# Self-attention projections in three rounded rounds, w2's sums behind attention, ternary clips split between VectorE and GpSimd

## The reference

```python
Xn = (X - mu) * rsqrt(var + LN_EPS) * ln_w + ln_b
Q, K, V = split(Xn @ W_in, 3);  Q, K = rope(Q), rope(K)      # 512 x 1536
out = softmax(Q K^T / sqrt(32)) V @ W_out + X
...
def act_quant(x):    # per token
    scale = 127.0 / clip(max(abs(x)), EPS); return clip(round(x * scale), -128, 127) / scale
def weight_quant(w): # one scale for a whole matrix
    scale = 1.0 / clip(mean(abs(w)), EPS);  return clip(round(w * scale), -1.0, 1.0) / scale
def bitlinear(x, w): return act_quant(x) @ weight_quant(w).T
h = silu(bitlinear(x, w1)) * bitlinear(x, w3);  return bitlinear(h, w2)   # 512 -> 1408 -> 512
```

## Time and profile before

| | us |
|---|---|
| median of 3 runs | 554.95 (554.63 to 555.12) |
| the profiled execution | 555.15 |
| its span, first to last instruction | 553.4 |
| PE busy in the span | 526.5 |
| DVE busy | 450.5 |
| ACT busy | 364.7 |
| POOL busy | 148.7 |

### The profile page before, as it was taken

One profiled execution on the slowest core, in us unless ns is written; L12 is line 12 of the kernel. 1 busy time (PEld: TensorE's weight loads), 2 busy tenths in 40 slices (PEclk: granted clock), 3 DMA queues, 4 the chain that ended last, 5 costly groups with the idle time before them and its releaser, 6 DMA issues.

```text
span 553.4 us, 10020 instructions
## 1 busy us (share of the span) xinstructions
PE 526.5 (95%) x3831; PEld 353.1 (64%) x3835; DVE 450.5 (81%) x650; ACT 364.7 (66%) x445; POOL 148.7 (27%) x202
## 2 busy tenths in 40 slices
PE   6989998799999999999999999999998899998996
PEld 3757763367666666767666676766677686454543
DVE  3354995999999999999999999999998833569686
ACT  2124535887887787788788688688688614995442
POOL 2367953002202202202202202202100001596500
PEclk9999999899999999999999999999999999999999
DMA  8999288999999999999999999999999987700001
GB/s 305 350 358 306 106 141 261 232 205 184 209 191 205 199 197 198 211 212 204 207 204 195 202 205 195 199 207 196 203 191 197 153 333 277 322 0 1 1 2 38
DMA packets 288350, 107.93 MB, mean 195 GB/s; under 512 B 276928, under 2 KB 278464, under 8 KB 286912
## 3 DMA queue, kind: packets, MB, share of 16 engines
q1 hardware_dynamic: 288320, 107.54, 89.6%
HBM read 37.79 MB, written 0.52 MB: 69 GB/s over the span
## 4 chain that ended last, share of the span: by engine, by line
PE 78%; DVE 10%; ACT 5%; DMA 4%; issue 2%; SPq 1%; ACTq 0%; DVEq 0%
PE ps L679 19%; PE ps L681 9%; PE ps L661 9%; PE ps L662 9%; PE ps L663 9%; PE ps L711 4%; PE ps L722 3%; DMA keys<-ctxT 2%; DVE rows L1300 2%; PE ps L788 2%; PE ps L733 2%; DVE split L1272 2%; PE ps L629 1%; PE ps L631 1%; PE ps L630 1%
## 5 line engine op out<-in xcount | busy, mean ns | idle before, releaser
L679 PE MATMUL ps<-pT,VH 128*128 128x256 f16 x1024 | 195.7, 273 | 3.7 <-DMA pT<-split 3.7
L681 PE MATMUL ps<-pT,VL 128*128 128x128 f16 x1024 | 182.6, 219 | 0.0
L1300 DVE TENSOR_SCALAR_CACHE_REDUCE rows<-ps,qback 128x1024 f32<-128x1024 f32 x128 | 163.6, 1280 | 17.8 <-PE ps L663 17.4
L1052 ACT ACTIVATE split<-rows,rz 128x2048 f16<-128x2048 f32 x64 | 124.6, 1995 | 67.7 <-DVE rz L1240 67.6
L1272 DVE SCALAR_TENSOR_TENSOR split<-rows,rz,split 128x2048 f16<-128x2048 f32 x64 | 150.1, 2348 | 2.9 <-ACT split L1052 2.1
L679 PEld LDWEIGHTS ps<-pT,VH 128*128 128x128 f16 x1024 | 100.4, 98 | 44.0 <-DMA pT<-split 5.7
L1038 ACT ACTIVATE rows<-rows,negm 128x2048 f32<-128x2048 f32 x64 | 127.2, 1988 | 0.2 <-DVE negm L1305 0.2
L681 PEld LDWEIGHTS ps<-pT,VL 128*128 128x128 f16 x1024 | 100.4, 98 | 27.3 <-issue 0.4
L542 POOL TENSOR_TENSOR ctx_c<-acc 128x128 f32<-128x128 f32 x32 | 23.9, 748 | 296.5 <-ACT acc L1027 296.5
L661 PE MATMUL ps<-KH,qcur 128*128 128x512 f16 x256 | 97.5, 381 | 3.3 <-DVE rows L1300 3.3
L662 PE MATMUL ps<-KL,qcur 128*128 128x512 f16 x256 | 97.5, 381 | 0.0
(11 more groups left out here) (187 smaller groups left out, 622.7 us busy)
## 6 DMA issues: line engine op xcount, KB each, us to landing
w_sb<-w SPq DMA_DIRECT2D x3, 2816.0 KB, 15.6
wq_sb<-wq SPq DMA_DIRECT2D x4, 1024.0 KB, 8.1
wo_sb<-wo SPq DMA_DIRECT2D x16, 256.0 KB, 5.3
wkcq_sb<-wkcq SPq DMA_DIRECT2D x4, 768.0 KB, 9.7
keys<-ctxT SPq DMA_DIRECT2D x8, 256.0 KB, 8.6
stage<-ctxT SPq DMA_DIRECT2D x16, 128.0 KB, 9.0
stage<-kcos SPq DMA_DIRECT2D x8, 256.0 KB, 9.1
stage<-ksin SPq DMA_DIRECT2D x8, 256.0 KB, 9.6
```

The source lines that it names most:

```text
L679: nc.tensor.matmul(bank(6 + r % 2, 0, 256), VH[:, 4 * b + k, :], p.rearrange("p x q -> p (x q)"), start=(b == 0 and k == 0), stop=False)
L681: last = nc.tensor.matmul(bank(6 + r % 2, 0, 128), VL[:, 4 * b + k, :], p[:, 0, :], start=False, stop=(b == 7 and k == 3))
L1052: nc.scalar.activation(split[:, split_slot(r, half), :, 0, :], rows[:, k, half * 2048:(half + 1) * 2048].rearrange("p (b k) -> p b k", k=1 ...
L1300: nc.vector.tensor_scalar(rows[:, k, c * 1024:(c + 1) * 1024], ps[:, score_bank(s) * 512:(score_bank(s) + 2) * 512], qback[:, r // 2:r // ...
```

## The change

The projections become three rounds on `float32r` operands. ScalarE rounds the three weights and the normalised tokens (`qkv_weight_high`, `normalised_high`), DVE subtracts for the low parts (`qkv_weight_low`, `normalised_low`), and DVE takes over scale and shift from ScalarE (`normalised`). TensorE's order becomes one of 72 products in groups (`project` with `highs` and `lows`). The loads of the key and query weights no longer wait for the last product of cross-attention, only for the last turned probabilities.

The residual of self-attention is rounded to a high and a low part on GpSimd, and added by two products with a rounded identity instead of an fp32 one.

The sums of w2 move from the time of the projections and scores to behind the last copy of probabilities, its total behind the last context, and its scale into the layer norm of tile 0, ahead of that norm's reciprocal. w1's clip on DVE becomes four quarters, one in each of the pairs 2 to 5, and w3's whole clip stands behind pair 5's context. w2's clip becomes eight pieces on GpSimd, two ahead of its multiplication for tile 0 of `hmid` and six behind it; each down product waits for its piece. GpSimd's wait for two clips and the ten dummy products are gone.

```diff
+    CLIPS = (4, 1)
...
-            sp.wait_ge(av_done, 16 * XH)
-            sp.dma_start(wink_sb[:, :, :], w_k).then_inc(win_in, 16)
-            sp.dma_start(winq_sb[:, :, :], w_q).then_inc(win_in, 16)
-            sp.dma_start(winv_sb[:, :, :], w_v).then_inc(win_in, 16)
+            for c in range(4):
+                sp.wait_ge(pt_in[c], 16 * 2 * XH)
+            sp.dma_start(wink_sb[:, :, :], w_k).then_inc(win_in[0], 16)
+            sp.dma_start(winq_sb[:, :, :], w_q).then_inc(win_in[1], 16)
+            sp.wait_ge(av_done, 16 * XH)
+            sp.dma_start(winv_sb[:, :, :], w_v).then_inc(win_in[2], 16)
...
+                nc.gpsimd.tensor_copy(x2hi[:, t, :], x_sb[:, t, :]).then_inc(x2hi_done, 1)
+                pool.wait_ge(x2hi_done, t + 1)
+                nc.gpsimd.tensor_tensor(x2lo[:, t, :], x_sb[:, t, :], x2hi[:, t, :].bitcast(f32), ALU.subtract)\
+                    .then_inc(x2lo_done, 1)
...
-            pool.wait_ge(wclip_done, 2)
             weight_magic(2, w2_sb)
             weight_round(2, w2_sb, w2b)
+            def last_clips(first, end):
+                for k in range(first, end):
+                    part = slice(k * DK * FF // WPIECES, (k + 1) * DK * FF // WPIECES)
+                    pool.wait_ge(wround_done, WPIECES * 2 + k + 1)
+                    nc.gpsimd.tensor_scalar(w2b[:, part], w2b[:, part], 1.0, -1.0, ALU.min, ALU.max).then_inc(w2clip_done, 1)
+
+            last_clips(0, 2)
             for t in range(TT):
                 a, b = HPARTS[1]
                 pool.wait_ge(hscale_done, t + 1)
                 nc.gpsimd.tensor_scalar(hmid[:, t, a:b], hmid[:, t, a:b], qscale[:, t:t + 1], MAGIC, ALU.mult, ALU.add)\
                     .then_inc(hmagic_done, 1)
+                if t == 0:
+                    last_clips(2, WPIECES)
...
-            project(0, 0)
+            project(0, 0, "weight", True, False)
             pe.wait_ge(x1_done, TT)
-            project(0, 1)
+            project(0, 1, "weight", True, False)
+            project(0, 0, "token", None, True)
+            project(0, 1, "token", None, True)
             pe.wait_ge(z1_done, 2)
             tile_transposes(z1[:, 1, :], 1, zT_done)
-            project(0, 2)
+            project(0, 2, "token", True, False)
+            project(1, 0, "weight", True, False)
+            project(0, 2, "weight", None, True)
+            project(1, 0, "token", None, True)
             weight_sum(0, bank(7, 0, 1))
-            project(1, 0)
-            project(1, 1)
...
-                if v == 2:
-                    weight_sum(2, bank(3, 0, 1))
+                if v == 0:
+                    pe.wait_ge(v_copied, 2)
+                    weight_sum(1, bank(3, 0, 1))
...
+                if t == 0:
+                    weight_sum(2, bank(0, 0, 1))
...
-            keep_busy(10, 2)
             quantised_transposes(0)
...
+                        if t == 0:
+                            pe.wait_ge(w2clip_done, -(-(c + 1) * DM // (DK * FF // WPIECES)))
...
+            for c in range(4):
+                abs_sum(2, c)
...
+            def qkv_weight_low(j):
+
+                dve.wait_ge(win_hi_done, j + 1)
+                nc.vector.tensor_tensor((wink_lo, winq_lo, winv_lo)[j][:, :, :].rearrange("p c d -> p (c d)"),
...
+            residual(0)
+            two_layernorms(0)
+            qkv_weight_low(0)
+            qkv_weight_low(1)
+            normalised(0)
+            normalised_low(0)
+            residual(1)
+            two_layernorms(1)
+            normalised(1)
+            qkv_weight_low(2)
+            normalised_low(1)
...
             rotate(0, 0)
+            rotate(0, 1)
             weight_total(0)
-            rotate(0, 1)
             value_copies(0)
+            rotate(1, 0)
             weight_scale(0, bank(7, 0, 1))
-            rotate(1, 0)
-            weight_total(1)
             rotate(1, 1)
-            weight_scale(1, bank(7, 0, 1))
...
-                if v in (2, 3):
-                    clip(v - 2, (w1b, w3b)[v - 2])
+                if v in (2, 3, 4, 5):
+                    clip(0, w1b, v - 2)
                 if v in (3, 5, 7):
                     context_out(v // 2 - 1)
+                if v == 5:
+                    clip(1, w3b, 0)
             context_out(FG - 1)
-            clip(2, w2b)
+            weight_total(2)
...
-                layernorm(x_sb, h2, t, t + 1, bank(6 + t), x3_done)
+                layernorm(x_sb, h2, t, t + 1, bank(6 + t), x3_done, between=(lambda: weight_scale(2, bank(0, 0, 1))) if t == 0 else None)
```

More of the change, by code:

```diff
@@ L152, in program @@
         acc = small("acc", [128, 2, 2, 128])
+        hTn_hi = at("hTn_hi", off[0], [128, TT, DK, 128], f32r)
         cT = small("cT", [128, FG, TOK])
@@ L291, in program @@
         warm_done = sem("warm_done")
-        wclip_done = sem("wclip_done")
-        win_in = sem("win_in")
+        wclip_done = [sem(f"wclip_done{k}") for k in range(2)]
+        w2clip_done = sem("w2clip_done")
+        identr_done = sem("identr_done")
+        x2hi_done = sem("x2hi_done")
+        x2lo_done = sem("x2lo_done")
+        win_hi_done = sem("win_hi_done")
+        win_in = [sem(f"win_in{k}") for k in range(3)]
+        win_lo_done = sem("win_lo_done")
         wkv_in = sem("wkv_in")
@@ L779, in weight_sum, with project @@
                 nc.tensor.matmul(dst, ones[:, :], wtot[:, j:j + 1], start=True, stop=True).then_inc(wsum_done, 1)
[L781 to L790 removed]
+            def project(t, j, lows, highs, final, chunks=range(DK)):
+                wh, wl = ((wink_hi, wink_lo), (winq_hi, winq_lo), (winv_hi, winv_lo))[j]
+                dst = bank(QKV_BANK[t][j])
+                if highs is not None:
+                    pe.wait_ge(win_hi_done, j + 1)
+                for c in chunks:
+                    if highs is not None:
+                        pe.wait_ge(hTn_hi_done, t + 1)
+                        last = nc.tensor.matmul(dst, hTn_hi[:, t, c, :], wh[:, c, :], start=(c == 0), stop=False)
+                    if lows in ("weight", "both"):
+                        pe.wait_ge(win_lo_done, j + 1)
+                        last = nc.tensor.matmul(dst, hTn_hi[:, t, c, :], wl[:, c, :], start=False,
+                                                stop=(final and lows == "weight" and c == DK - 1))
+                    if lows in ("token", "both"):
+                        pe.wait_ge(hTn_lo_done, t + 1)
+                        last = nc.tensor.matmul(dst, hTn_lo[t][:, c, :], wh[:, c, :], start=False,
+                                                stop=(final and c == DK - 1))
+                if final and c == DK - 1:
@@ L813, in _ @@
-            project(1, 2, range(DK // 2, DK))
+            project(1, 1, "both", True, True)
+            for j in range(2):
+                pe.wait_ge(rot_done, j + 1)
+                tile_transposes(qkn[:, 0, j, :], 2 if j == 1 else 0, qkT_done)
+            pe.wait_ge(v_copied, 1)
+            project(1, 2, "both", True, False, range(DK - 1))
+            pe.wait_ge(rot_done, 3)
+            tile_transposes(qkn[:, 1, 0, :], 1, qkT_done)
+            project(1, 2, "both", True, True, range(DK - 1, DK))
@@ L1182, in _, with layernorm @@
             roots, variances = [0], [0]
-            def layernorm(src, dst, first=0, end=TT, in_psum=None, copied=None):
+            def layernorm(src, dst, first=0, end=TT, in_psum=None, copied=None, between=None):
                 tiles = slice(first, end)
@@ L1199, in layernorm @@
                 dve.wait_ge(dve_chain, chain[0])
+                if between is not None:
+                    between()
                 dve.wait_ge(sd_done, roots[0])
```

118 lines of the change are left out of this document (65 added, 53 removed).

## The result

The changed kernel takes 563.79 us (median of 6 runs) against 555.29 for the kernel before (6 runs beside it): ratio 1.0143, 95% interval 1.0119 to 1.0167. It is slower by some 8 us. The forecast had the sign and its range held the time, but its 574.5 was 11 us too long. The profiled execution took 564.8 us, its span 563.0.

The account below looks back on a forecast made before the run. Late chain: TensorE up to self-attention's scores, DVE from 500 to 508 us, then DVE, ScalarE and TensorE in turn. 14.3 + 0.3 + 4.4 + 0.6 = 19.6 us on a 553.4 span, 1.75 around it, less 0.2: 574.5 us, range 563 to 581.

Parts of the forecast that it names:

- the 14.3 us: Feed-forward part: DVE's normalisation of tile 0 waits out GpSimd's w2 stream, ending at 539.6 instead of 525.30.
- Rival B: DVE gets in behind each GpSimd piece, as rotations do: about 553.5 us (550 to 557), chance 0.11.
- The clip in parts: Attention: first quarter of w1b's clip stands some 8 us until GpSimd's stream ends; last copy of probabilities 1.2 us late.
- The clock: Feed-forward part: after idling, TensorE runs w1b's products at 1.2 GHz, +1.7 us; another slow stretch in tile 1's hidden work, +0.6.
- No dummies: Ahead of the feed-forward part: tile 0's transposes no longer wait for dummy products, -1.4 us.
- Sums of w2: Behind self-attention: last layer norm's statistics start at 523.4 instead of 522.57, GpSimd begins on w2 at 525.2.
- six clip pieces: Behind GpSimd's multiplication for tile 0: DVE's first hb operation waits 4.4 us more (bounds 2.4 and 5.0).
- Projections: Ahead of self-attention's scores: 72 products, 0.227 us each, take 4.3 us less; 2.0 kept (bounds 0 and 4.3).

Follow-up runs that it names:

- experiments 2 to 5: Mostly the changed kernel, often with late clips, with a min/max or wait added on DVE; the float32 min/max took 6.90 us behind pair 4's maxima, 0.67 in w2's stream.
- experiment 1: Changed kernel with w1b's clip moved behind w3b's (555.44 us), or with TensorE products that add zero while the clip stands (560.21 us).
- b_early: Kernel before without fill products, w1b's clip in halves behind the copies of pairs 0 and 1, w3b's behind pair 6's maxima: 555.26 us, ratio 1.0002.
- b_nodummy: Kernel before without the ten products that fill TensorE ahead of the feed-forward part: 553.89 us, ratio 0.9975.
- e_late: Changed kernel with w1b's four clip quarters moved behind w3b's clip, when GpSimd has no stream: 555.44 us, ratio 0.9992.
- b_late: Kernel before with w1b's clip moved behind pair 5's maxima, right ahead of w3b's: 555.97 us, ratio 1.0006.
- b_open: b_early with GpSimd's w2 stream no longer waiting for the clips, against the kernel before: 551.88 us, ratio 0.9924.
- e_door: e_late with float32 min/max operations on DVE behind the maxima of pairs 1, 2, 3 and 4: 555.86 us, single run.

## Why the prediction was right and wrong

*The step that failed* is the 14.3 us: "DVE's normalisation of tile 0 ... finds it running, and ends 0.3 us after it". The normalisation found the stream running, and took 1.07 us instead of 0.55. I had sorted by the form of the operation, rotations that get in and clips that don't; experiments 2 to 5 showed one and the same float32 operation stand 6.90 us in one place and get in at others, so its form did not decide. Rival B's mechanism held in the feed-forward part, the forecast's in attention. The trace of before held the difference: the rotations come within 3.7 us of a pause or of each other, the clip 15.7 us after DVE's last entry.

That the range held the time is luck: 14.3 and 4.4 of its 19.6 us were laid on the feed-forward part, which lost 2.5, and most of the loss came in attention.

*The clip in parts* stood about as forecast (6.85 us, some 8 expected) and ended 0.4 us behind the stream, as forecast. Its price was not. Attention was to begin 2.0 us sooner and end 1.2 later, 3.2 longer; it is 5.6 longer. The term left out TensorE, whose clock was granted at 0.50 behind the idle time of the stall (3.3 us in experiment 1).

*The clock* was put in the wrong place: +1.7 for w1b's products and +0.6 in the hidden layer. TensorE's idle time ahead of tile 0's transposes was 2.14 us, not 14, the granted clock stayed at 1.00, and neither term is there. In b_early, where it idled 2.85 us at that place and the clock fell, w1b's products took 1.4 us more, near the 1.7 forecast. *No dummies*, -1.4: measured -1.4 in b_nodummy.

*Sums of w2 and six clip pieces.* These cost 3.9 us together (37.41 against the 33.55 of b_nodummy, which has no fill products either). About 3.3 are the shares of a piece that h, the quantisation, h2b and cw lose in two tiles; the clip pieces, 4.4 in the forecast, hold the second hb operation up by 0.6. The down products wait 0.35 for one of them, but from hb on the end comes no later than in b_nodummy (10.6 us in both).

*Projections* kept 0.5 us of 2.0, within the bounds. The products run one every 0.23 us as forecast, and the wait for w1's total is there:

```profile
480.31 0.38 PE L816 MATMUL ps<-wtot,ones 128*128 128x1 f32 x2 [1.15 <-DVE wtot L1510]
...
482.03 0.40 PE L827 MATMUL ps<-winq_hi,hTn_hi 128*128 128x512 f32 x1
482.27 0.39 PE L830 MATMUL ps<-winq_lo,hTn_hi 128*128 128x512 f32 x1
```

The direction was right for half the reason: the stalled clip alone (8.2 us) makes the change slower, and without it (e_late, ratio 0.9992) the rest is worth nothing either way.

## What to carry to other kernels

Two operations that differ in behaviour differ in more than their form: before sorting them, list for each what ran on the other engine and for how long, and when the waiting engine last got through. Where GpSimd works in long streams of pieces, put DVE's SBUF operations near its last entry or behind a pause, not late in the stream. A gain in one stage has to be followed to the next wait: b_early and b_late lost all of theirs there, and b_open got it by taking that wait away too.

## What the runs showed of the hardware

DVE operations from SBUF to SBUF got in behind the running GpSimd piece when GpSimd had run up to 13 pieces (10.9 us) since DVE's last entry, or had paused 2.7 us; from 17 pieces without a pause (14.4 us) on they stood in every case until the stream ended, up to 9 pieces. An entry starts the count anew (e_door, a single run). Above a count of 5 without a pause every entry was between scaling pieces, and all that stood met rounding pieces. So where the limit lies for either sort of piece, whether it counts pieces or time, and what in the chip keeps it, these runs don't tell. Operations that read PSUM kept their length in the same stretches (maxima 1.20 to 1.23 us).

The Trainium skill (SBUF — State Buffer, Who interferes with whom) has whoever issues first hold the shared ports for the whole instruction. The entries up to 13 pieces agree, with waits of one piece at most; the clip that stood through 9 pieces, issued before eight of them, does not.
